# Mask of 9 of 12 self-attention score tiles copied by ScalarE into three buffers, 30 idle products in the prologue, and the cross queries moved ahead in the middle chain

## The reference, cut to what matters

```python
x = x + self_attention(layernorm(x))        # causal, 16 query heads, 4 key/value heads of 16, rotary
x = x + cross_attention(layernorm(x), ctx)  # 16 heads of 16, one mask for all batches and heads
x = x + feed_forward(layernorm(x))          # 256 -> 1024 -> 256, hidden and w2 rounded to 8-bit floats
# self_attention
q = rope(h @ Wqa @ Wqb); k, v = split(h @ Wkva @ Wkvb); k = rope(k)
scores = where(key > query, -inf, q @ k.T * scale)
out = softmax(scores) @ v @ Wout + bout
```

## Time and profile before

| | |
|---|---|
| median of 3 runs | 1766.15 us (1763.48 to 1766.48) |
| profiled execution, its time | 1764.05 us |
| its span | 1762.4 us |
| PE busy | 1630.8 us (93%), 11950 matmuls |
| weight loads busy (PEld) | 970.7 us (55%) |
| DVE / ACT / POOL busy | 1160.1 / 1114.2 / 754.4 us (66 / 63 / 43%) |
| mean granted TensorE clock | 0.982 |

### The profile page before, as it was taken

How to read it: one execution, slowest core, us unless ns; L and a number is a source line. 1 busy time by engine, 2 the same in 40 slices (tenths; PEclk the granted TensorE clock), 3 DMA queues, 4 the chain that set the end, 5 groups by cost and what they waited for, 6 DMA issues and landing times.

```text
span 1762.4 us, 33722 instructions
## 1 busy us (share of the span) xinstructions
PE 1630.8 (93%) x11950; PEld 970.7 (55%) x11950; DVE 1160.1 (66%) x1736; ACT 1114.2 (63%) x1733; POOL 754.4 (43%) x1010
## 2 busy tenths in 40 slices
PE   3869999999999999999999999999999999999988
PEld 2435555656555565555656555565655656555555
DVE  4467485775848668485775848667584766848573
ACT  4455675756668565675756568575666856567574
POOL 2252344644345453444544334453434545344410
PEclk7879999999999999999999999999999999999999
DMA  7464453754546364543845546374454636454330
GB/s 179 57 92 71 64 87 64 101 93 62 94 58 105 67 93 82 72 90 52 119 70 77 91 62 93 64 100 90 66 93 55 107 68 90 85 69 83 54 46 12
DMA packets 106238, 140.17 MB, mean 80 GB/s; under 512 B 12385, under 2 KB 74242, under 8 KB 105954
## 3 DMA queue, kind: packets, MB, share of 16 engines
q1 hardware_dynamic: 103090, 130.96, 47.9%
q0 software_dynamic: 2352, 8.26, 1.5%
q10 hardware_dynamic: 768, 0.57, 0.1%
HBM read 21.29 MB, written 8.39 MB: 17 GB/s over the span
## 4 chain that ended last, share of the span: by engine, by line
PE 54%; issue 15%; DVE 11%; POOL 7%; ACT 7%; DMA 5%; POOLq 0%; SPq 0%; ACTq 0%; DVEq 0%
PE o_pair L1459 9%; PE score L1420 5%; PE small L1290 5%; DVE negmax L1022 4%; PE small L1544 4%; DMA Q<-negT 3%; PE small L1306 3%; PE o_pair L1290 3%; DVE P L1054 3%; PE score L1397 2%; PE small L1578 2%; PE small L1472 2%; POOL x L527 2%; PE score L1402 2%; ACT P L780 2%
## 5 line engine op out<-in xcount | busy, mean ns | idle before, releaser
L1022 DVE TENSOR_REDUCE negmax<-score 128x4 f32<-128x1024 f32 (+1 forms) x384 | 456.5, 1214 | 41.9 <-PE score L1378 21.9
L780 ACT ACTIVATE P<-score 128x1024 f32<-128x1024 f32 x448 | 446.3, 1026 | 50.4 <-PE score L1426 25.2
L1459 PE MATMUL o_pair<-P,V 128*32 128x256 f32 (+1 forms) x4096 | 280.0, 362 | 2.4 <-DVE P L1054 2.4
L1054 DVE TENSOR_TENSOR P<-P,cross_bound 128x1024 f32<-128x1024 f32 x192 | 231.4, 1248 | 70.0 <-ACT P L780 69.4
L830 ACT ACTIVATE score<-cross_q 128x1024 f32<-128x1024 bf16 x192 | 196.3, 1023 | 54.6 <-DVE negmax L1022 53.3
L1459 PEld LDWEIGHTS o_pair<-P,V 128*32 128x32 f32 x4096 | 87.8, 108 | 133.5 <-issue 79.8
L1420 PE MATMUL score<-Q,K 99*128 99x256 bf16 x1024 | 152.7, 276 | 7.5 <-DMA Q<-negT 6.3
L1578 PE MATMUL small<-xnT,w 128*128 128x256 f32 x600 | 156.7, 379 | 0.0
L558 POOL TENSOR_TENSOR x<-x,ffn 128x1024 f32<-128x1024 f32 x15 | 32.8, 2188 | 269.5 <-DVE negmax L1022 269.5
L1378 PE MATMUL score<-K,Q 96*128 96x256 bf16 x768 | 118.8, 278 | 28.6 <-ACT score L830 23.6
L1420 PEld LDWEIGHTS score<-Q,K 99*128 99x128 bf16 x1024 | 82.5, 98 | 109.1 <-ACT P L780 63.0
(11 more groups left out here) (199 smaller groups left out, 3076.1 us busy)
## 6 DMA issues: line engine op xcount, KB each, us to landing
K<-k2p SPq DMA_DIRECT2D x96, 256.0 KB, 6.2
Q<-q2p SPq DMA_DIRECT2D x192, 128.0 KB, 4.7
Q<-q1p SPq DMA_DIRECT2D x90, 256.0 KB, 6.2
x_in<-in_x SPq DMA_DIRECT2D x16, 512.0 KB, 5.3
ctxT<-in_ctx SPq DMA_DIRECT2D x16, 512.0 KB, 5.7
k2f<-q1f SPq DMA_DIRECT2D x32, 256.0 KB, 6.0
inT<-o_sb SPq DMA_DIRECT2D x60, 128.0 KB
o<-inverse SPq DMA_DIRECT2D x60, 128.0 KB
```

The source lines that it names most:

```text
L780: A.activation(P[:, t % 4, :], score[b][:, :, :], ACT.Exp, scale=SCALE).then_inc(score_free[b], 1)
L1022: V.tensor_reduce(negmax[:, k, h:h + 1024 // w], s.rearrange("p (h w) -> p h w", w=w), AX.X, ALU.max, negate=True).then_inc(score_free[b], 1)
L1054: V.tensor_tensor(p, p, cross_bound[:, t % 2, :].unsqueeze(1).broadcast_to([128, 4, SEQ]), ALU.min).then_inc(probs_masked[1], 1)
L1459: last = T.matmul(o_ps[ob][32 * j:32 * j + 32, SEQ * gg + q0:SEQ * gg + SEQ], v, p, start=s == 0, stop=end, tile_position=(0, 32 * j), ski ...
```

## The change

- `self_scores` uses three buffers in turn (`self_tile`: t % 3, the third is `o_pair`). Tiles 0, 1, 2 keep the mask products on TensorE; for tiles 3 to 11 ScalarE copies the mask into the buffer (`self_premask`) and TensorE's products add to it. Tile 2 waits until both outputs of `times_v` have been copied out of `o_pair`.
- ScalarE's list holds nine `self_premask` between its other steps; `cut_first(0, i, 0)` and `cut_second(0, i, 0)` stand behind the masks of tiles 7 and 8, and `maxima(0, 0)` behind that of tile 10.
- TensorE: `v2_0` goes ahead of and behind tile 2, `k2_1` one tile forward, `v2_1` into the maxima pass around tile 7; `out2_1` goes behind tile 1 of the exponential pass, where `v2_1` was.
- The middle chain: `xnT2_1` directly behind `query1(st, 1)`, `query2(st, 1)` ahead of `key1`, h2 split around `value1`. VectorE: `norm_apply` of batch 1 ahead of `query2_third(i, 0)`, and `query2_third(i, 1)` ahead of the maxima pass, no more behind its first tile. ScalarE's list follows.
- Prologue: 30 products of 512 columns (identity times identity) into `small[0]` ahead of the `bias` products.

```diff
-PROLOGUE = ["xnT1_0", "xnT1_1", "qa", "q0", "q1", "k", "v_0", "v_1", "maskT", "boundT", "bias"]
+PROLOGUE = ["xnT1_0", "xnT1_1", "qa", "q0", "q1", "k", "v_0", "v_1", "maskT", "boundT", "warm0", "bias"]
...
-    attention = (["k2_0"] + p("m2T_1") + ["v2_0", "k2_1", "m1T_0"] + p("out2_0", "out2_1")
-                 + ["v2_1", "m1T_1", "o1t0", "o1t1", "oT1_0", "o1t2"])
+    attention = (["k2_0"] + p("m2T_1") + ["v2_0", "k2_1", "v2_1", "m1T_0"] + p("out2_0", "out2_1")
+                 + ["m1T_1", "o1t0", "o1t1", "oT1_0", "o1t2"])
-              + n("qa") + ["xnT2_0", "out1_1", "q2_0"] + n("q0") + p("h1") + n("q1", "k") + p("h2")
-              + ["xnT2_1"] + n("v_0", "v_1") + ["q2_1"])
+              + n("qa") + ["xnT2_0", "out1_1", "q2_0"] + n("q0") + p("h1") + n("q1") + ["xnT2_1", "q2_1"]
+              + n("k") + p("h2") + n("v_0", "v_1"))
...
+        def self_tile(g, t):
+            n = t % 3
+            return n, g * (TILES // 2 if n < 2 else SELF_USES + CROSS_USES[2]) + t // 3
...
+            def self_premask(g, t):
+                n, before = self_tile(g, t)
+                act.wait_ge(score_free[n], before)
+                if t % 6 < 4:
+                    A.activation(bufs[n][:, :, :].rearrange("p c (j k) -> p (c j) k", j=2),
+                                 causal_q[:, :].unsqueeze(1).broadcast_to([128, 4, SEQ]),
+                                 ACT.Copy).then_inc(masked[n], 1)
+                else:
+                    A.activation(bufs[n][:, :, :].rearrange("p c (j k) -> p (c j) k", j=4),
+                                 causal_q[:, 128:256].unsqueeze(1).broadcast_to([128, 8, 128]),
+                                 ACT.Copy).then_inc(masked[n], 1)
...
+                self_premask(i, 3)
+                self_premask(i, 4)
                 values2(st, 0)
-                cut_first(0, i, 0)
-                cut_second(0, i, 0)
+                self_premask(i, 5)
+                self_premask(i, 6)
                 keys(st, 1)
                 keys_full(st, 1)
+                self_premask(i, 7)
+                cut_first(0, i, 0)
+                self_premask(i, 8)
+                cut_second(0, i, 0)
+                self_premask(i, 9)
+                values2(st, 1)
+                self_premask(i, 10)
+                maxima(st, 0, 0)
+                self_premask(i, 11)
                 keys_second(st, i, 0)
-                maxima(st, 0, 0)
                 keys_second(st, i, 1)
...
                 query2_second(st, 0)
                 if nxt:
                     turn(st, "q1", q1f[:, 1, :])
+                turn_batch(st, "xnT2_1", 1, inT)
                 premask(i, 0)
                 if prev:
                     hidden(st, [1])
+                query2_first(st, i, 1)
                 if nxt:
                     turn(st, "k", k1f[:, :], rows=KV_HEADS * HD)
+                query2_second(st, 1)
+                premask(i, 1)
+                if nxt:
+                    values1(st)
                 if prev:
                     hidden(st, [2])
-                turn_batch(st, "xnT2_1", 1, inT)
-                if nxt:
-                    values1(st)
-                premask(i, 1)
-                query2_first(st, i, 1)
-                query2_second(st, 1)
...
+                norm_apply(1, x2, GB * i + 1, range(2, 4))
                 query2_third(i, 0)
-                norm_apply(1, x2, GB * i + 1, range(2, 4))
                 query2_rest(st, i, 1)
+                query2_third(i, 1)
                 for t in range(N2):
                     row_max(1, i, t)
-                    if t == 0:
-                        query2_third(i, 1)
...
+                    by_pe = t < SELF_PE_MASKED
+                    if not by_pe:
+                        _, use = masked_use("S1", g, t)
+                        pe.wait_ge(masked[n], use + 1)
+                    elif n == 2:
+                        for ob in range(2):
+                            if positive(g * UNITS):
+                                pe.wait_ge(o_free[ob], g * UNITS)
+                    elif positive(before):
                         pe.wait_ge(score_free[n], before)
...
-                    if t == 1 and a == 0:
-                        tokens(st, "v2", ctxT, wv2, 1)
+                    if t == 1 and out2:
+                        pe.wait_ge(o2_whole, GB * g)
+                        tokens(st, "out2", inT, wo2, 1)
...
+            def warm(st, name, n):
+                bk = st.bank(name)
+                pe.wait_ge(small_free[bk], st.before(name))
+                for k in range(n):
+                    last = T.matmul(small[bk][:, :], identb[:, :], again(identb, 4), start=True, stop=True)
+                    if k == 0:
+                        last.then_inc(small_full[bk], 1)
+                last.then_inc(small_free[bk], 1)
...
+            warm(PRO, "warm0", 30)
             bk = PRO.bank("bias")
...
+                tokens(st, "v2", ctxT, wv2, 0, 0)
+                self_scores(i, [2])
+                tokens(st, "v2", ctxT, wv2, 0, 1)
                 self_scores(i, [3])
                 self_scores(i, [4])
-                tokens(st, "v2", ctxT, wv2, 0, 0)
+                key2(st, 1, 0)
                 self_scores(i, [5])
-                tokens(st, "v2", ctxT, wv2, 0, 1)
+                key2(st, 1, 1)
                 self_scores(i, [6])
-                key2(st, 1, 0)
+                tokens(st, "v2", ctxT, wv2, 1, 0)
                 self_scores(i, [7])
-                key2(st, 1, 1)
+                tokens(st, "v2", ctxT, wv2, 1, 1)
                 self_scores(i, [8])
                 turn_max(st, 0, i, 0)
                 self_scores(i, [9])
                 self_scores(i, [10])
                 self_scores(i, [11])
                 if prev:
-                    for r in range(2):
-                        pe.wait_ge(o2_whole, GB * (i - 1) + r + 1)
-                        tokens(st, "out2", inT, wo2, r)
+                    pe.wait_ge(o2_whole, GB * (i - 1) + 1)
+                    tokens(st, "out2", inT, wo2, 0)
...
                 if nxt:
                     query1(st, 1)
-                if prev:
-                    hidden_half(st, 1, 1)
-                if nxt:
-                    key1(st)
-                if prev:
-                    hidden_half(st, 2, 0)
-                    hidden_half(st, 2, 1)
                 pe.wait_ge(xn_ready[1], GB * i + 2)
                 turned_batch(st, "xnT2_1", 1, xn)
+                if prev:
+                    hidden_half(st, 1, 1)
+                batch_copied(st, "xnT2_1")
+                query2(st, 1)
+                if nxt:
+                    key1(st)
+                if prev:
+                    hidden_half(st, 2, 0)
                 if nxt:
                     for r in range(2):
                         value1(st, r)
-                batch_copied(st, "xnT2_1")
-                query2(st, 1)
+                if prev:
+                    hidden_half(st, 2, 1)
```

More of the change, by code:

```diff
@@ L662, in body @@
                     if nxt:
-                        n, before = tile("S1", i + 1, 0)
+                        n, before = self_tile(i + 1, 0)
                         pool.wait_ge(score_free[n], before + 1)
@@ L734, in cut_first @@
                 last = N1 // GB * (b + 1) - 1
-                for t in (last, last - 1) if a == 0 else last_cross_tiles(b):
-                    n, before = tile("S1", g, t) if a == 0 else cross_tile(g, t)
+                for t in (last, last - 1, last - 2) if a == 0 else last_cross_tiles(b):
+                    n, before = self_tile(g, t) if a == 0 else cross_tile(g, t)
                     act.wait_ge(score_free[n], before + 1)
@@ L1012, in row_max @@
             def row_max(a, g, t):
-                b, before = tile("S1", g, t) if a == 0 else cross_tile(g, t)
+                b, before = self_tile(g, t) if a == 0 else cross_tile(g, t)
                 dve.wait_ge(score_full[b], before + 1)
-                s = (score[b] if a == 0 else cross_bufs[b])[:, :, :].rearrange("p c n -> p (c n)")
+                s = bufs[b][:, :, :].rearrange("p c n -> p (c n)")
                 if a == 0 and t % 6 >= 4:
@@ L1377, in cross_scores @@
                             h = 4 * hg + 2 * c + j
-                            last = T.matmul(cross_bufs[n][:, c, SEQ * j:SEQ * j + SEQ],
+                            last = T.matmul(bufs[n][:, c, SEQ * j:SEQ * j + SEQ],
                                             Q2[0:KROWS, b, h, 128 * (k % 2):128 * (k % 2) + 128],
@@ L1382, in cross_scores @@
                     for c in range(2) if t in PE_MASKED else ():
[L1383 removed]
+                        last = T.matmul(bufs[n][:, c, :], identb[:, :], again(cross_q[:, k % 2, :], 2),
                                         start=False, stop=True, skip_group_check=True)
@@ L1439, in times_v @@
                         pe.wait_ge(small_free[2 + ob], st.opened(2 + ob))
-                        n, before = cross_tile(g, 11)
+                    if u < 2:
```

(1 more changed line is left out.)

78 lines of the change are left out of this document (37 added, 41 removed).

## The result

| | before | after |
|---|---|---|
| median | 1765.77 us (4 runs) | 1736.38 us (1735.51 to 1739.84, 4 runs) |
| ratio | | 0.9839, 95% interval 0.9822 to 0.9856 |
| profiled execution, span | 1764.05, 1762.4 | 1737.21, 1735.6 |

The account below looks back on a forecast made before the run. TensorE, 93% busy, was taken as dense except for stalls in and behind the self maxima pass and in the cross maxima pass. 1764.05 - 18 - 18 + 1 = 1729 profiled, 1731 median, stated 1732; range 1714 to 1762.

Parts of the forecast that it names:

- the forecast's own spread: Whole kernel: the forecast case, a time of 1723 to 1741 us, chance 0.45.
- Part 2: Self pass, `v2_1` and `out2_1` moved: exponential of tile 2 starts 1.2 us earlier per body, 18 us with the masks.
- Part 3: Middle chain and cross maxima pass: negated maxima issued 1.8 us earlier, 1.3 us gained in each of 14 bodies, 18 us.
- Part 4: Prologue, 30 idle products: later start, full clock regains some; 1 us lost once, bounds 2 gained and 5 lost.
- Part 1: Self maxima pass, nine masks moved to ScalarE: 2.78 us of products per body, worth nothing alone but room for other work.
- Its cover: GpSimd's 1.36 us wait before `keys_rest` was to absorb `cut_third` coming 1.3 us later, with no slack.
- `add_bias2` unmoved: GpSimd behind the self maxima pass: `add_bias2` still ends near 908.6; a later end would be wrong.
- The slower rival: Self maxima pass: masks waiting for `row_max` hold `cut_second` 2.5 us longer; 1787 us, chance 0.12.
- its upper bound: Self pass, `v2_1` and `out2_1` moved: 1.7 us per body if only the products count.
- a sign of being wrong: Cross maxima pass: a copy of maxima that takes over 6 us.
- the copy stays where it is: Cross maxima pass: negated maxima's copy held by its queue place; 18 us gained, 1 lost, 1749; chance 0.20.
- The second page: Skill page against a gain: weight loads' share, 55%, would make TensorE look half free and its products worth nothing.

Follow-up runs that it names:

- part 3 alone: The kernel before with only the middle chain's new order (second query batch ahead, VectorE's rotation after it); 1761.03 us, ratio 0.9965.
- the best kernel: The change plus nine idle products in self maxima waits, one stacking copy behind the maxima copy, GpSimd's cut ahead of the keys' third part; 1704.71 us, ratio 0.9658.
- e9_two_ahead: The changed kernel with one of three query stacking copies moved behind the middle's first maxima copy, two left ahead; 1728.75 us, ratio 0.9787.

## Why the prediction was right, and where it wasn't

**The sum**: 35 us off the profiled execution were forecast, 26.8 came; the time lies in the forecast's own spread, in part by luck. Over all bodies the parts gave this. Part 2, the self pass of bodies 1 to 15: 21.6 us for 18. Part 3, their cross maxima pass: 2.9 us for 18, since bodies 1 and 15, taken as gaining or at nothing, lost 1.9 and 1.7 of the 6.5. Part 4, body 0 with its start: 3.6 us gained for 1 lost. The end of the kernel gave 1.5 that no part named, and the other two stretches of bodies 1 to 15 took back 2.9. So the failure of part 3 (15 us) was half made good by terms that were off the other way.

**Part 1, right.** `row_max` 2 was to lose 0.9 us: 0.98. `row_max` 11 was to end 17.0 us behind the start of the first (906.6 - 889.65): 893.13 - 876.15 = 17.0. `cut_third` 1.3 us later in the body: 11.13 for 10.07 from that start, 1.1. Its cover, the 1.36 us ahead of `keys_rest`, is gone as said. `add_bias2` unmoved: it ends 18.7 us behind that start, 19.0 before. The slower rival (ScalarE's list) didn't come: `cut_second` of the first half had room.

**Part 2, right in mechanism, mis-sized.** 1.2 us a body; measured 1.7 in eight bodies (its upper bound) and 0.6 in five, 1.3 in the mean. In a good body 0.3 of the 1.7 come from GpSimd's chain, which lets `cut_second` go 18.9 us behind the first `row_max` and not 19.2. What was missing in the working is the granted clock: it was taken as full behind the prologue.

**Part 3, the term that failed.** "I take 1.3, nearer to the upper, since the issue itself moves by 1.8": the issue moved by 1.87, but 0.5 us arrived. The copy then takes 6.26 us, over the 6 that the prediction named as a sign of being wrong. The value taken weighed the wrong row: it held the copy's 4.8 us to be nearly its own. The chain up to the issue was right (GpSimd's cut at 948.71 without waiting, no mask waits but one of 0.23), but the copy's duration is not its own: TensorE's start hangs on the first stacking copy, 10.1 us behind it in four kernels (before, the change, the copy from ScalarE's queue, part 3 alone); with two of them ahead it is at most 8.3 (945.99 to 954.32, without a wait). The windows show the DMA engines' share full meanwhile, in the change from 950 on:

```profile
950.00:952.00 2.00, 1.47 (x11) 0.68 (x10) 1.98 (x3) 2.00 (x4) 2.00 (x2) 1.00 1.05 171
952.00:954.00 2.00, 2.00 (x20) 1.79 (x19) 1.26 (x2) 1.63 (x3) 2.00 (x6) 1.00 1.05 115
954.00:956.00 2.00, 2.00 (x18) 1.38 (x17) 1.81 (x2) 1.38 (x2) 2.00 (x2) 1.00 1.05 113
```

At 115 GB/s the 768 KB take 6.8 of the 10.1 us; what fills the rest no run shows. What moved was only the first stacking copy, by 0.5 us, and that is the gain. The rival "the copy stays where it is" was nearly right on what the copy gains, not on the reason that it gave ("its place in the queue"), and its total (1749) was too high because part 2 and body 0 gave more. The Trainium skill's rule on order in one queue ("DMA: Bandwidth & Descriptors", section "Two DMAs through the same engine are not ordered") pointed the right way, but the run from another queue shows that the queue isn't what binds. The same page of the Trainium skill, section "Queues, rings and completion order", says that a copy's semaphore write lands only after every earlier write of that DMA engine, across its queues; the 10.1 us from either queue agree with that.

**Part 4, wrong in kind.** "I take 1 us lost, once": tile 0 started 0.56 us later at clock 1.00, which held to 60 us (it was 0.50 from 110 to 130). Body 0's first stretch is 24.12 us with the products ahead, 25.56 without any, 26.44 with them elsewhere, 27.93 before. But tile 0 starts anywhere between 41.94 and 44.65 us in the ten kernels that have them ahead, and at 41.20 and 43.23 in the two that don't. The third exponential of body 0 starts at 66.48 us in the change and at 66.76 without any idle products. So as a warm-up their worth isn't shown, not even its sign. Their worth in the code, 117 us, was in no row: the trace of before has a loop that fits.

**The second page** ("Perfetto Trace Analysis" of the Trainium skill, weight loads for how full TensorE is): from the change to the best kernel TensorE's products rose from 11692 to 11831 and the weight loads' share from 55 to 56%, and the time fell by 32 us, so it was waits that went. That doesn't contradict the page. What products are worth where TensorE is dense no run tested.

## What to carry to other kernels

A transfer that "takes 4.8 us" may be waiting for those issued before it: measure from the earlier ones, and if the end keeps its distance to them, move copies from ahead of it to behind it, not its own issue. When a wait goes and the time stays, look at the next engine's list at that place; here the same 1.5 us lay behind it, and one more move gave 18.6 us. And read the instruction loads on the profile's page after any edit to a looped kernel: a few instructions more or fewer ahead of the loop can cost more than the edit gains; 60 fewer cost 117 us here, and the change had gained 29.

## What the runs showed of the hardware that I hadn't expected

- A loop of TensorE that is loaded anew in each turn: 9 blocks fetched per turn, 6 us of waiting at the jump and the lower clock behind it, 9 us a turn in all; with 60 instructions more ahead of it, none.
- The reader of a copy of 24 KB behind 768 KB starts 10.1 us after the first of these is issued, whether from the same queue or another; behind 512 KB within 8.3.
- The granted clock falls in some bodies and not in others at the same waits (clock 0.84 and 1.00 in the windows above). Which ones stays open; with products in the waits it fell in none of bodies 2 to 14, and in one kernel without them (`e9_two_ahead`) in none either. After 2.5 us of waiting for a copy (body 1) it was 0.76 in 232 to 238.
